# Two gathered experts in place of four combined, and short quads in the last two phases

## The reference, cut to what matters

```
x: [32, 32, 32, 64] float32                      # 32 images, 64 channels
x = x + L0(group_norm(x));  x = x + L1(group_norm(x))

L0 (three steps, K = 4 experts, TOP_N = 2):
    k, v    = x @ Wk, x @ Wv
    attn    = softmax over pixels of q.k ;  pooled = attn.v
    weights = softmax(where(allowed, pooled @ Wmlp, -1e9) / 1.5)
    top_vals, top_idx = top_k(weights, 2)
    wsel    = weights * one_hot(top_idx), divided by its sum     # two of four are not zero
    x_mod   = x * (1 + mean over heads of attn * S * softplus(alpha))
    x       = sum over e of wsel[e] * (conv3x3(x_mod, We[e]) + be[e])
    allowed = allowed without top1 (the last expert stays allowed)

L1: an involution: a 1x1 reduction, a 1x1 expansion to 9 weights per group and pixel,
    the weighted sum of the 9 shifted projections
```

## Time and profile before

| what | value |
|---|---|
| median of 3 runs | 683.7 us (682.75 to 683.96) |
| span of the profiled execution | 680.8 us |
| TensorE busy | 649.5 us (95%) |
| VectorE busy | 553.8 us (81%) |
| ScalarE busy | 285.0 us (42%) |
| GpSimd busy | 172.3 us (25%) |
| DMA in the 40 slices | 9 tenths in the first two, then 0 to 2 tenths |

### The profile page before, as it was taken

The page is one execution under the profiler, slowest core; times in us unless marked ns, Lnnn a source line. Parts: engine busy times, 40 slices in busy tenths (PEclk is TensorE's granted clock), DMA queues, the critical chain, the costliest instruction groups (busy, mean ns, idle before and its releaser), DMA issues.

```text
span 680.8 us, 14823 instructions
## 1 busy us (share of the span) xinstructions
PE 649.5 (95%) x6176; PEld 268.1 (39%) x6176; DVE 553.8 (81%) x904; ACT 285.0 (42%) x367; POOL 172.3 (25%) x156
## 2 busy tenths in 40 slices
PE   7878999999999999999999999999999999999995
PEld 7433333333333333333333334433445444444442
DVE  5698866989988988995577787849888888888885
ACT  3753622322331322133002411033676777777661
POOL 2100310009102800550051110411353243244230
PEclk9979999999999999999999999998999999999998
DMA  9920000000000000000000000000111211121122
GB/s 332 213 56 1 2 1 1 1 1 2 2 1 1 2 1 1 2 1 1 1 14 2 1 1 2 1 1 1 32 33 32 58 37 33 45 49 33 32 62 63
DMA packets 54511, 19.67 MB, mean 29 GB/s; under 512 B 51154, under 2 KB 51892, under 8 KB 54452
## 3 DMA queue, kind: packets, MB, share of 16 engines
q1 hardware_dynamic: 54164, 18.57, 11.2%
q10 hardware_dynamic: 288, 0.21, 0.1%
HBM read 10.39 MB, written 8.39 MB: 28 GB/s over the span
## 4 chain that ended last, share of the span: by engine, by line
PE 74%; DVE 15%; issue 1%; ACT 1%; DVEq 0%; ACTq 0%
PE conv L675 35%; PE att L745 11%; PE conv L729 10%; PE att L465 4%; PE conv L641 4%; PE att L544 4%; DVE xpad L1188 3%; DVE comb L1277 2%; PE att L717 2%; DVE stats L1291 2%; PE att L556 2%; DVE x L1497 2%; PE att L523 1%; DVE x L1246 1%; DVE x L1253 1%
## 5 line engine op out<-in xcount | busy, mean ns | idle before, releaser
L675 PE MATMUL conv<-xpad,comb 64*64 64x512 f32 x2592 | 290.3, 595 | 3.1 <-DVE x L1253 2.9
L1497 DVE TENSOR_TENSOR x<-conv,x 128x512 f32<-128x512 f32 x288 | 179.2, 683 | 26.4 <-PE conv L729 25.0
L675 PEld LDWEIGHTS conv<-xpad,comb 64*64 64x64 f32 x2592 | 99.3, 134 | 170.1 <-issue 159.4
L1277 DVE SCALAR_TENSOR_TENSOR comb<-experts,wsel,comb 128x576 f32<-128x576 f32 (+1 forms) x138 | 113.5, 888 | 5.2 <-ACT comb L857 4.8
L729 PE MATMUL conv<-rstack,wse 98*128 98x512 f32 x288 | 96.2, 444 | 1.9 <-DVE xin L1286 0.9
L857 ACT ACTIVATE comb<-experts,wsel 128x576 f32<-128x576 f32 (+2 forms) x49 | 35.2, 768 | 108.5 <-PE conv L675 69.7
L745 PE MATMUL att<-x,cmp 64*32 64x512 f32 x1280 | 79.7, 596 | 0.0
L729 PEld LDWEIGHTS conv<-rstack,wse 98*128 98x128 f32 x288 | 49.5, 189 | 60.7 <-DVE x L1497 46.2
L1188 DVE SCALAR_TENSOR_TENSOR xpad<-att,x 128x1024 f32<-128x1024 f32 x46 | 54.0, 1215 | 20.8 <-PE att L523 20.6
L1634 POOL TENSOR_TENSOR x<-x,xin 128x1024 f32<-128x1024 f32 x15 | 35.9, 2396 | 115.1 <-ACT x L997 115.1
L867 ACT ACTIVATE x<-conv,bias 128x512 f32<-128x512 f32 x40 | 25.2, 680 | 84.0 <-PE conv L675 84.0
(11 more groups left out here) (187 smaller groups left out, 611.4 us busy)
## 6 DMA issues: line engine op xcount, KB each, us to landing
x<-in_x SPq DMA_DIRECT2D x32, 256.0 KB, 5.1
out<-comb SPq DMA_DIRECT2D x30, 256.0 KB, 3.2
experts<-in_We SPq DMA_DIRECT2D x1, 1152.0 KB
out<-comb SPq DMA_DIRECT2D x4, 128.0 KB, 2.2
wide<-in_c_wide SPq DMA_DIRECT2D x1, 192.0 KB, 5.9
x<-in_c_sum SPq DMA_DIRECT2D x1, 160.0 KB
small<-in_c_small ACTq DMA_DIRECT2D x1, 142.5 KB, 3.8
map_sel<-in_c_map SPq DMA_DIRECT2D x1, 128.0 KB
```

What stands on the lines that cost most here:

```text
L675: last = nc.tensor.matmul(conv[own[to], h, HW * rows:HW * rows + HW], comb[own[rows], q % 2, n, tap(t)], xpad[own[rows], 2 * (q % 2) + n, ...
L1277: v.scalar_tensor_tensor(comb[:, q % 2, n, cols], experts[:, e, cols], wsel[:, p % 2, j + QP * n, e:e + 1], comb[:, q % 2, n, cols], ALU.m ...
L1497: v.tensor_tensor(img(prod[i])[:, rows, :], img(conv[:, unit, :])[:, rows, :], xip[s][:, kh + 16 * h:kh + 16 * h + 16, kw:kw + W], ALU.mul ...
```

## The change

- Row forms: GpSimd makes a fourth block, `plus - middle` (`minus_forms`), and SyncE writes all forms of the four experts to a table in HBM (`forms`, 64 channels by 7 blocks of 192 columns for each expert).
- Routing also gives, for each pair of images and each of its two ranks, the expert's number (`top_at`, whole numbers in SBUF) and its weight (`top_weight`): on VectorE for phase 1 (`pick_experts`, 7 instructions after `route(1)`), on GpSimd for phases 2 to 5 (10 more instructions in `route_beside`).
- From quad 5 on (`GATHER_FROM`), SyncE fetches the two chosen experts of each image of the next quad from the table: 8 values are loaded to registers and 8 copies issued, each 64 partitions by 576 or 768 columns. They land in `chosen`, which is the old `experts` tile (one buffer), so each gather waits for `comb_added` of the quad before.
- `begin_combine` takes rank 0 from `chosen`, `combine_two` adds rank 1: two steps on VectorE for a quad, not six.
- `SHORT` also holds places 0 and 2 of phases 4 and 5. Such a quad writes its rows to `x` (in phase 5 to two spare slots) and `finish_rows` completes them; GpSimd adds them to the residual (`add_residual`), and `final_stats` waits for that. `final` is left for the full quads, which VectorE still empties in phases 4 and 5.
- SyncE's `LATE_CONSTS` now wait for the residual of quad 18, and stand between the gathers of quads 20 and 21.
- The second group norm's average moves from the second half of quad 22 into the last stage of its short form.

```diff
-SHORT = tuple(QP * p + j for p in range(1, LAST) for j in (0, 2))
+SHORT = tuple(QP * p + j for p in range(1, PHASES) for j in (0, 2))
+GATHER_FROM = QP + 1
 # SyncE
-            modulated(eng, QP * LAST + 2)
+            def gather(q):
+                p, j = divmod(q, QP)
+                if j == 0 or q == GATHER_FROM:
+                    eng.wait_ge(top_ready, p)
+                first, size = (0, 4 * ROW) if q in SHORT else (4 * ROW, TAPS * C)
+                for n in range(2):
...
+                        eng.wait_ge(comb_added[n], added(q - 1))
+                    for m in range(2):
+                        for r in range(TOP):
+                            at = eng.value_load(top_at[64 * m:64 * m + 1, p % 2, j + QP * n, r:r + 1], min_val=0, max_val=K - 1)
+                            eng.dma_start(chosen[own[m], n, r, 0:size],
+                                          forms[bass.ds(at, 1), :, first:first + size].rearrange("k p c -> (k p) c")).then_inc(gathered[n], 16)
+            write_forms()
+            eng.wait_ge(forms_out, 16 * FORMS_WRITTEN)
+            for q in range(GATHER_FROM, QP * LAST + 5):
+                gather(q)
+            eng.wait_ge(residual_added, residuals(QP * LAST + 2))
             for dst, src in LATE_CONSTS:
                 eng.dma_start(dst, src).then_inc(late_consts_in, 16)
+            for q in range(QP * LAST + 5, QUADS):
+                gather(q)
 # ScalarE, begin_combine
+                        if q >= GATHER_FROM:
+                            eng.wait_ge(gathered[n], 64 * (q - GATHER_FROM + 1))
+                            first, weight = chosen[:, n, 0, cols], top_weight[:, p % 2, j + QP * n, 0:1]
 # VectorE
+            def pick_experts(p):
+                ranked = [128, GP, TOP, K]
+                own_rank, taken, half = cmp[:, 0, :, 0:TOP, :], cmp[:, 1, :, 0:TOP, :], cmp[:, 2, :, 0:TOP, 0:2]
+                pk = Steps(eng, pick_step)
+                v.tensor_scalar(own_rank[:, :, 0, :], rt[:, 5, :, :], 0.5, None, ALU.is_lt)
+                pk.then(v.tensor_scalar(own_rank[:, :, 1, :], rt[:, 5, :, :], 1.0, None, ALU.is_equal))
+                pk.then(v.tensor_tensor(taken, own_rank, ramp.unsqueeze(1).unsqueeze(1).to_broadcast(ranked), ALU.mult))
+                pk.then(v.tensor_tensor(half, taken[:, :, :, 0:2], taken[:, :, :, 2:4], ALU.add))
+                v.tensor_tensor(top_at[:, p % 2, :, :], half[:, :, :, 0], half[:, :, :, 1], ALU.add).then_inc(top_ready, 1)
+                eng.wait_ge(top_ready, p)
+                pk.then(v.tensor_tensor(taken, own_rank, bc(wsel[:, p % 2, :, :], 2, ranked), ALU.mult))
+                v.tensor_reduce(top_weight[:, p % 2, :, :], taken, AX.X, ALU.add).then_inc(top_weighed, 1)
 # VectorE, combine_two
+                for n in range(2):
...
+                    v.scalar_tensor_tensor(comb[:, q % 2, n, cols], chosen[:, n, 1, cols], weight(n, 1),
                                            comb[:, q % 2, n, cols], ALU.mult, ALU.add).then_inc(comb_added[n], 1)
 # VectorE, the order
             route(1)
+            pick_experts(1)
             next_mask_and_bias(1)
             combine(4)
...
-                    if q - 1 >= QP * LAST:
-                        final(q - 1, 1)
                     if q - 1 in SHORT:
                         finish_rows(q - 1, 1)
+                    elif q - 1 >= QP * LAST:
+                        final(q - 1, 1)
...
-                        combine(q + 1)
+                        combine_two(q + 1)
...
-                    if q >= QP * LAST:
+                    if q >= QP * LAST and q not in SHORT:
                         final(q, 0)
 # GpSimd
+            def add_residual(q):
+                eng.wait_ge(short_emptied, 2 * SHORT.index(q) + 2)
+                first = slot(q, 0) if q < QP * (PHASES - 1) else SPARE
+                for n in range(2):
+                    v.tensor_tensor(xin[:, slot(q, n), :], xin[:, slot(q, n), :], x[:, first + QP * n, :], ALU.add)\
+                        .then_inc(residual_added, 1)
...
-            for p in range(2, PHASES):
+            for p in range(2, PHASES - 1):
                 route_beside(p)
+            add_residual(QP * LAST)
+            route_beside(PHASES - 1)
+            add_residual(QP * LAST + 2)
```

More of the change, by code:

```diff
@@ L178, in build @@
         rpar = rpar[0:AR, :]
+        ramp = packed(small, (4 + K) * D + 29, K)
+        top_at = packed(small, 0, 2 * GP * TOP).bitcast(mybir.dt.int32).rearrange("p (a i r) -> p a i r", a=2, r=TOP)
+        top_weight = packed(small, 2 * GP * TOP, 2 * GP * TOP).rearrange("p (a i r) -> p a i r", a=2, r=TOP)
+        chosen = experts[:, :, :].rearrange("p (n r) c -> p n r c", n=2)
+        minus_forms = row_sums[:, :, :, :, :].rearrange("p a b c d -> p (a b c d)")[:, 0:K * ROW].rearrange("p (k c) -> p k c", k=K)
+        forms = nc.dram_tensor("forms", (K, C, FORM_BLOCKS * ROW), F32, kind="Internal")
         pair_avg, same_image = (packed(wide, n * 128, 128) for n in range(2))
@@ L337, in rows_of, with hurried_upto, added @@
         def rows_of(q, h):
-            first = slot(q, 0)
+            first = slot(q, 0) if q < QP * (PHASES - 1) else SPARE
             return x[:, first:first + QP + 1:QP, :].rearrange("p n (r e c) -> p n r e c", e=2, c=W)[:, :, :, h, :]
         def hurried(q):
-            return q - 1 in SHORT and q % QP == QP - 1
+            return q - 1 in SHORT and q % QP == QP - 1 and q < QP * LAST
+        def hurried_upto(q):
+            return sum(hurried(k) for k in range(q + 1))
+        def added(q):
+            return (K - 1) * (2 + min(q, GATHER_FROM - 1) + 1) + max(0, q - GATHER_FROM + 1)
         def modulated(eng, q):
@@ L1262, in combine @@
                 cols = slice(0, 4 * ROW if q in SHORT else TAPS * C)
+                for e in range(1, K):
+                    for n in range(2):
+                        if e > 1:
+                            eng.wait_ge(comb_added[n], (K - 1) * (2 + q) + e - 1)
+                        else:
+                            eng.wait_ge(comb_begun[n], 2 + q + 1)
+                        v.scalar_tensor_tensor(comb[:, q % 2, n, cols], experts[:, e, cols], wsel[:, p % 2, j + QP * n, e:e + 1],
+                                               comb[:, q % 2, n, cols], ALU.mult, ALU.add).then_inc(comb_added[n], 1)
@@ L1263, in combine, with combine_two, weight @@
+            def combine_two(q):
+                p, j = divmod(q, QP)
+                cols = slice(0, 4 * ROW if q in SHORT else TAPS * C)
+                def weight(n, r):
+                    return top_weight[:, p % 2, j + QP * n, r:r + 1]
                 if hurried(q):
                     eng.wait_ge(conv_full, sections(q - 2, 1))
-                    v.tensor_scalar(comb[:, q % 2, 0, cols], experts[:, 0, cols], wsel[:, p % 2, j, 0:1], None, ALU.mult)\
+                    eng.wait_ge(gathered[0], 64 * (q - GATHER_FROM + 1))
+                    v.tensor_scalar(comb[:, q % 2, 0, cols], chosen[:, 0, 0, cols], weight(0, 0), None, ALU.mult)\
@@ L1266, in combine @@
                         .then_inc(own_begun, 1)
[L1267 to L1277 removed]
+                for n in range(2):
+                    if hurried(q) and n == 0:
+                        eng.wait_ge(own_begun, hurried_upto(q))
+                    else:
+                        eng.wait_ge(comb_begun[n], 2 + q + 1 - (0 if n else hurried_upto(q - 1)))
+                    v.scalar_tensor_tensor(comb[:, q % 2, n, cols], chosen[:, n, 1, cols], weight(n, 1),
@@ L1562, in row_forms @@
                 v.tensor_scalar(plus, plus, 0.5, None, ALU.mult).then_inc(forms_ready, 1)
+                eng.wait_ge(forms_ready, 3)
+                eng.wait_ge(shift_full, 1)
+                v.tensor_tensor(minus_forms[:, :, :], plus, middle, ALU.subtract).then_inc(forms_ready, 1)
             def bc(ap, axis, shape):
```

118 lines of the change are left out of this document (82 added, 36 removed).

## The result

| what | before | after |
|---|---|---|
| median, measured side by side | 683.23 us (682.68 to 683.96) | 689.85 us (689.43 to 690.66) |
| ratio, with its 95% interval | | 1.0103 (1.0089 to 1.0118) |
| span of the profiled execution | 680.8 us | 688.0 us |
| start of quad 8 on TensorE | 193.62 | 197.84 |
| start of quad 16 (ScalarE's row) | 320.60 | 324.83 |

The change makes the kernel 1% slower; 677.6 us was forecast. The time is inside the range, the sign is wrong. 4.2 us are lost before quad 8, nothing between quads 8 and 16, and 3.4 us more in phases 4 and 5, where the forecast had a gain of 7.75 us.

What follows compares the result with a forecast made beforehand. TensorE, busy for 95% of the span, was taken as the bound. The terms -8.1 + 0.2 + 1.5 + 0.1 + 0.15 = -6.15 us took 683.7 to 677.6 us, with a range of 670 to 692 us.

Steps and rivals of the forecast that it cites:

- Part 1: Short form in phase 4: quads 16 and 18 take 19.1 and 11.75 us like quads 8 and 10, together -8.1 us.
- Part 2: Short form in phase 5: 8.1 us of TensorE work saved, all given back through VectorE's order; +0.2 us in sum.
- T19: Start of quad 19, from which the forecast walks VectorE; quad 20 was to start 19.9 us later.
- T21: Start of quad 21 in that walk, forecast 33.1 us after quad 19's start, against 31.9 before the change.
- Part 5: Gather on SP: 1.1 us for a pair of load and copy; +0.1 us at quad 5, +0.15 at quad 21.
- T23: Start of quad 23 in that walk, forecast 28.8 us after quad 21's start.
- Part 3: `pick_experts(1)` on VectorE ahead of quad 4: seven small operations of 0.22 us, uncovered, +1.5 us.
- Part 4: Two experts combined, not four: VectorE saves some 3 to 4 us per quad, worth nothing to TensorE in phases 1 to 4.
- Rival 1: Register loads set the pace: at s us a pair, quads 5 and 21 lose 8(s - 1.1) each; slower, chance 0.25.
- Rival 2: VectorE keeps up in phase 5, for instance through less combining, so its 8.1 us are gained too: 669.2 us, chance 0.15.

Runs made afterwards that it cites:

- run 2: Changed kernel with GpSimd's residual additions for the short quads of phases 4 and 5 cut to one column, the rest left out: 686.97 us, ratio 1.007.
- run 6: Changed kernel with GpSimd's residual additions of quads 18 and 20 and two late constant steps moved later, VectorE's order kept: 685.51 us, ratio 1.0039.
- run 4: Changed kernel with only VectorE's order altered in phases 4 and 5, `final` and the statistics moved: 683.77 us, ratio 1.0015.
- run 9: Changed kernel with GpSimd's long steps moved, VectorE reordered, quad 5 combined from four experts, quad 20's residual and the statistics placed earlier: 671.27 us, ratio 0.9827.
- run 12: Kernel of run 9 with the gather only from quad 17 on, phases 1 to 3 combining four experts: 668.21 us, ratio 0.9784.
- run 3: Changed kernel without the loads of register values, the copies always fetching experts 0 and 1: 686.1 us, ratio 1.0056.
- run 11: Kernel of run 9 with GpSimd's residual additions of quads 18 and 20 put back to start as soon as rows are there: 671.5 us, ratio 0.9833.

## Why the prediction was wrong, point by point

- **Part 1, right for the quads, a wait was missed.** Quads 16 and 18 take 19.13 us (324.58 to 343.71) and 11.80 us, as forecast. But quad 17 takes 17.59 us and not 16.38, since quad 18 waits for `final(17, 0)`. The order alone doesn't make this wait, as run 2 shows. In the change VectorE's two small routing steps stand beside the residual addition of quad 16 and take 0.99 and 2.29 us instead of 0.18 and 0.19. No term has this: +1.2 us.
- **Part 2, the step that failed: the walk from T19 to T21, 39.9 us for 33.1.** It gave every VectorE step its length alone, and every wait of TensorE no price but its own length. The order that it walks through is right: run 6 has that order, and from T19 on VectorE's steps have their lengths alone there. `final(19, 0)` begins at T19+18.5 (391.62 - 373.11) as forecast, quad 20 starts at T19+20.2 for 19.9, and quad 21 (407.40) at T19+34.3 for 33.1. In the change `combine_two(20)` was 4.2 us longer, so `modulate(20)` (387.62) began at T19+14.5 instead of 11.1; `subtract_rows` was 2.3 us longer, so `final(19, 0)` began at T19+24.2 instead of 18.5. The residual additions stand in Part 5 at "two pairs at 2.4", with no thought of whom they run beside. Order and collisions both hold quad 20: it starts 25.9 us after quad 19 in the change, 19.7 with the order alone mended (run 4), 20.2 with GpSimd's places alone mended (run 6), and 16.05 with both (run 9). From T21 to T23 30.5 us were measured for 28.8 (quad 22 waits at its start too), and the norm in quad 23 held TensorE 2.20 us where 2.4 was forecast.
- **The price of a wait was taken as its length.** Stretches of the kernel after the change, each with one of TensorE's waits at its start or just ahead of it; the columns are the stretch, its length, the busy time of TensorE with its instructions, its granted clock as a share of 2.4 GHz, and the DMA's share and GB/s:

```profile
130.00:137.00 7.00, 5.50 (x44) 0.76 0.35 102
...
387.00:395.00 8.00, 7.40 (x56) 0.79 0.28 77
...
399.00:407.00 8.00, 8.00 (x52) 0.66 0.16 51
...
452.00:467.00 15.00, 14.97 (x110) 0.89 0.00 0
```

  TensorE waits 2.53 us ahead of quad 4, 3.19 in quad 19, 4.56 ahead of quad 20 and 2.20 in quad 23. Behind each the mean clock lies between the levels of 1.2 GHz (0.5) and 2.4 GHz (1.00); from 137 to 147, 343 to 387 and 407 to 452 it was 1.00, and in the kernel before it was 1.00 from 343 to 458. The matmuls there are slower: 8 and 32 in quad 4 take 1.79 and 4.30 us, 1.09 and 3.64 before; 48 in quad 19 take 7.04 and 48 in quad 20 8.09, 5.33 in run 9, where they come after no such wait; 4 in quad 23 take 3.41, 1.96 before. That is 1.4 + 1.7 + 2.8 + 1.45, some 7.3 us in all, more than half of what the forecast was off by. Of the 12.5 us that quads 19 and 20 take over run 9's 27.4, 7.75 are waits and 4.5 this. The prediction put it at nothing. Not every wait has this behind it: after 1.60 us in quad 22, 16 matmuls take 1.97 us in run 9 and 3.64 in run 12.
- **Part 3, near.** Quad 4 waits 2.53 us for VectorE in place of 1.33: 1.2 us for a forecast of 1.5. With the slower matmuls behind that wait it is 2.6.
- **Part 4, right in phases 1 to 3.** Run 12 combines four experts there, and these phases are as long as before.
- **Part 5, the term mis-sized.** A pair takes 1.5 us, not 1.1. The rows of a pair add up to 0.354 + 0.152 + 0.018 + 0.046 + 0.029 + 0.469 = 1.07 us, which is the estimate; the other 0.43 us lies between the rows, and only start to start shows it. Rival 1's price for quad 5, 8(s - 1.1), gives 3.2 us with s = 1.5, and quad 4 lost 22.45 - 19.28 = 3.2 us (131.15 to 153.60 after, 130.10 to 149.38 before). That the two agree is luck: without the loads quad 4 still loses 1.5 us (run 3), so they cost 1.7, about half of the price. The other half of rival 1, the same loss in quad 21, doesn't show: the landing that ScalarE waits for comes at T19+28.0 (401.09) for a forecast of 25.0, 1.4 us of it because the residual of quad 18 is late (T19+10.6 for 9.2), but quad 20 is so late itself that `combine_two(21)` (403.00) waits for no landing. The Trainium skill, DMA: Bandwidth & Descriptors, section Latency and other measured facts, has a `tensor_load` at about 600 ns at least. The row here is shorter, with a median of 354 ns, and run 3 puts all that a load adds to a pair at 0.9 us.
- **The sum.** The forecast span was 674.65 us and the profile's 688.0, 13.35 more. The terms: quad 4 +3.1, quad 17 +1.2, T19 to T21 +6.8, T21 to T23 +1.7, quad 23 +1.6 (466.24 - 443.5 = 22.7 for 21.1), Part 3 -0.3, and Part 5's 0.15 for quad 21 not needed. That is +13.95; -0.6 is left over, 0.4 of it in L1, which is that much shorter.
- **Rival 2**, 669.2 us, is near what other kernels reach, the mended ones (671.27 and 668.21). Its saving is there to be had, but not for its reason: VectorE doesn't keep up by having less to do, its order and GpSimd's places must change.

How the 15.9 us that phases 4 and 5 gain between the change and run 9 (141.41 and 125.56) divide among order, collisions and late residuals can't be told by adding: order alone gives 6, GpSimd's moves alone give 4.4 with a new wait of 4.39, and run 11 shows that with the right order two of the collisions cost some 1 us or nothing. A collision costs what VectorE is behind already. What `subtract_rows` loses to lines 1751 and 1753 under the right order wasn't tried.

## What to carry to other kernels

When a unit of work gets shorter, walk the engine that empties it through every quad where the pattern occurs, and give each of its steps the length that it has beside what the other engines will then be doing. A helper engine's work is free only in a place where it neither lengthens a step of an engine that is late nor holds a buffer that someone reuses. Where TensorE sets the time, price a wait of it by the matmuls behind it too: here four waits made them 7.3 us longer. An estimate that comes out right can still be luck: the loads' 3.2 us in quad 4 were two causes of about half that each. A gain that vanishes may still be there: here the same short quads were worth 12.9 us as soon as the orders around them were mended, and a gather that saved VectorE work in phases where VectorE wasn't late only brought its waits.
